# Three of seven replicated tiles of the first chunk made by matmuls with a zero-one matrix instead of transferred

## The reference

```
e = stack([tbl_f[ids[:, f]] for f in range(39)], axis=1)      # 512 x 39 x 16
x0 = xk = e
for W, b in layers:                                            # three layers, 128 wide
    z = relu(einsum('bhd,bkd,hks->bsd', x0, xk, W) + b)
    xk, rest = z[:, :64], z[:, 64:]                            # rest goes to the output
z = sum over d of the rests and of the last z                  # 512 x 256
h = relu([z, dense_ctx] @ W_top1 + b_top1)                     # 512 x 512
y = relu(h @ W_top2 + b_top2) @ W_top3                         # 512 x 1
```

## Time and profile before

| | |
|---|---|
| median of three runs | 650.6 us |
| profiled execution | 650.27 us, span 648.4 us |
| PE busy | 610.6 us (94%), 2008 instructions |
| DVE busy | 562.3 us (87%) |
| POOL busy | 535.9 us (83%) |
| ACT busy | 409.4 us (63%) |
| DMA | 90.30 MB, mean 139 GB/s |

### The profile page before, as it was taken

The page is one execution under the profiler, slowest core; times in us unless marked ns, Lnnn a source line. Parts: engine busy times, 40 slices in busy tenths (PEclk is TensorE's granted clock), DMA queues, the critical chain, the costliest instruction groups (busy, mean ns, idle before and its releaser), DMA issues. The chain is left out here.

```text
span 648.4 us, 6323 instructions
## 1 busy us (share of the span) xinstructions
PE 610.6 (94%) x2008; PEld 377.5 (58%) x2008; DVE 562.3 (87%) x637; ACT 409.4 (63%) x551; POOL 535.9 (83%) x326
## 2 busy tenths in 40 slices
PE   4269899999999999999999999999999999999998
PEld 1126466656666566656656566656666665665554
DVE  1469898998989898998999898998989898988973
ACT  2135758577766758576766758576766758585533
POOL 6778799998989899998989899998989896865550
PEclk9978999999999999999999999999999999999999
DMA  6689554738364655648373546648373545620000
GB/s 228 153 194 272 141 156 100 230 79 247 73 204 107 192 155 132 198 84 247 72 224 83 170 113 131 199 78 252 72 227 90 177 96 140 186 65 1 0 0 2
DMA packets 64044, 90.30 MB, mean 139 GB/s; under 512 B 46624, under 2 KB 49568, under 8 KB 60042
## 3 DMA queue, kind: packets, MB, share of 16 engines
q1 hardware_dynamic: 57506, 88.29, 50.1%
q0 software_dynamic: 5120, 1.29, 2.1%
q10 hardware_dynamic: 1384, 0.32, 0.2%
HBM read 87.31 MB, written 8.95 MB: 148 GB/s over the span
## 5 line engine op out<-in xcount | busy, mean ns | idle before, releaser
L398 POOL TENSOR_TENSOR low<-prod,high 128x1024 fp32r<-128x1024 f32 (+1 forms) x160 | 381.0, 2399 | 54.3 <-ACT high L469 53.0
L643 DVE TENSOR_TENSOR prod<-spread,x 128x1024 f32<-128x1024 f32 x256 | 308.0, 1214 | 32.8 <-ACT x L489 29.1
L759 PE MATMUL z<-prod,w_sb 128*128 128x512 f32 (+2 forms) x608 | 290.8, 599 | 18.6 <-DVE prod L624 14.0
L469 ACT ACTIVATE high<-prod 128x1024 fp32r<-128x1024 f32 (+1 forms) x160 | 168.0, 1058 | 118.1 <-DVE prod L643 100.6
L776 PE MATMUL z<-high,high_w_L 128*128 128x512 f32 (+1 forms) x448 | 203.3, 454 | 5.3 <-ACT high L479 4.3
L791 PE MATMUL z<-low,high_w_L 128*128 128x512 f32 (+1 forms) x448 | 182.8, 489 | 4.3 <-POOL low L398 2.9
L388 POOL DMA_INDIRECT gat<-table_dram,index x160 | 154.0, 962 | 36.5 <-issue 33.9
L776 PE MATMUL z<-high,low_w_L 128*128 128x512 f32 (+1 forms) x448 | 177.9, 397 | 0.0
L759 PEld LDWEIGHTS z<-prod,w_sb 128*128 128x128 f32 (+2 forms) x608 | 115.7, 191 | 105.6 <-issue 85.2
L791 PEld LDWEIGHTS z<-low,high_w_L 128*128 128x128 f32 (+1 forms) x448 | 82.4, 189 | 70.5 <-issue 45.7
L489 ACT ACTIVATE x<-z,bias_sb 64x512 f32<-64x512 f32 (+1 forms) x174 | 112.4, 646 | 13.2 <-PE z L759 6.9
(11 more groups left out here) (48 smaller groups left out, 104.0 us busy)
## 6 DMA issues: line engine op xcount, KB each, us to landing
spread<-x_rows SPq DMA_DIRECT2D x15, 1792.0 KB, 7.2
spread<-x_rows SPq DMA_DIRECT2D x32, 768.0 KB, 12.6
spread<-x_rows SPq DMA_DIRECT2D x16, 1024.0 KB, 7.3
x_rows<-x_rows SPq DMA_DIRECT2D x16, 390.0 KB
x0base<-x_rows SPq DMA_DIRECT2D x47, 78.0 KB
gat<-table_dram,index POOLq DMA_INDIRECT x160, 3.4
x_rows<-gat SPq DMA_DIRECT2D x31, 72.0 KB
wt_sb<-wt_dram SPq DMA_DIRECT2D x2, 512.0 KB, 4.3
```

The costliest lines, as they stand in the source:

```text
L398: pool.tensor_tensor(low[0:rows, h, 0:k, :], prod[0:rows, slot(c, kind, g), 0:k, :], high[0:rows, h, 0:k, :].bitcast(F32), ALU.subtract).t ...
L469: act.activation(high[0:rows, split_slot(c, kind, g), 0:k, :], prod[0:rows, slot(c, kind, g), 0:k, :], ACT.Copy).then_inc(high_ready, 1)
L643: dve.tensor_tensor(prod[0:rows, slot(c, kind, g), :, :], spread[0:rows, c % 2, g, :].unsqueeze(1).to_broadcast([rows, k, N]), x[0:rows, : ...
L759: last = pe.matmul(z[:, :], w[0:rows, at + j, :], prod[0:rows, slot(c, kind, g), j, :], start=g == 0 and j == 0, stop=closes and j == k - 1)
```

## The change

The lot of tiles 0-1 is not transferred, nor is tile 6. `FIRST_CUTS` is now two lots, tiles 2-3 and 4-5. A matrix `select` of zeros and ones (39 rows by three times 117 columns, 54.8 KB) is loaded at the start into a corner of `spread`. After the context matmuls TensorE waits for it, for VectorE to have taken the context sums out of `x1` and `x2`, and for `x0base`, and makes tiles 0, 1 and 6 from the first 39 rows of `x0base` by one matmul each, into `x1` (two halves) and `x2`. VectorE multiplies groups 0 and 3 of the first chunk from there, with `x0base` itself as the other factor in place of its copy `base`.

```diff
-FIRST_CUTS = ((0, 2), (2, 4), (4, T0))
+FIRST_CUTS = ((2, 4), (4, 6))
+SELECTED = (0, 1, 6)
...
+        select_sb = spread[0:F, 1, n1 + n2:G1, :].rearrange("p g n -> p (g n)")[:, 0:len(SELECTED) * R0]
...
+        selected = {t: (x1[0:R0, 0, :], x1[0:R0, 1, :], x2[0:R0, 0, :])[n] for n, t in enumerate(SELECTED)}
...
             def load_base(c, js=range(DPT)):
...
+                    if c == 1:
+                        sp.wait_ge(prod_done, PROD_NUMBER[0, "L0", G0 - 1])
...
             def load_spread(c, p):
...
                 if c == 1 and p == 0:
                     sp.wait_ge(low_w_ready, 3)
+                    sp.wait_ge(select_done, len(SELECTED))
...
             sp.dma_start(bt1_sb[:, :], bt1).then_inc(ctx_in, 16)
+            sp.dma_start(select_sb, select).then_inc(select_in, 16)
             sp.dma_start(w1_part, w1_split).then_inc(w1_in, 16)
...
             def product0(c, g):
-                if g == 0:
+                if g == (1 if c == 0 else 0):
                     dve.wait_ge(base_ready, c + 1)
-                    if c >= 1:
-                        dve.wait_ge(spread0_in, 16 * c)
+                if c >= 1 and g == 0:
+                    dve.wait_ge(spread0_in, 16 * c)
...
+                x0, other = spread0[0:rows, 2 * g:2 * g + k, :], base
+                if c == 0 and 2 * g in SELECTED:
+                    dve.wait_ge(base_in, 16 * DPT)
+                    dve.wait_ge(select_done, 1 + SELECTED.index(2 * g + k - 1))
+                    x0 = x1[0:rows, 0:k, :] if g == 0 else x2[0:rows, 0:k, :]
+                    other = x0base
...
+            pe.wait_ge(select_in, 16)
+            pe.wait_ge(ctx_taken, H1 // P)
+            pe.wait_ge(base_in, 16 * DPT)
+            for n, t in enumerate(SELECTED):
+                pe.matmul(selected[t], select_sb[:, n * R0:(n + 1) * R0], x0base[0:F, :],
+                          start=True, stop=True).then_inc(select_done, 1)
             pe.wait_ge(w1_in, 32)
...
+def selection():
+    out = np.zeros((F, len(SELECTED), R0), np.float32)
+    rows = np.arange(R0)
+    for n, t in enumerate(SELECTED):
+        out[(rows % F + t) % F, n, rows] = 1
+    return out.reshape(F, len(SELECTED) * R0)
```

More of the change, by code:

```diff
@@ L148, in stage_end, with tower_kernel @@
     return max(DONE[c, kind, g] for g in range(G0 if kind == "L0" else G1))
-def tower_kernel(nc, ids, offsets, table, w0a, w0b, w1, w1_split, w2, w2_split, biases, wt1, bt1, wt2, bt2, wt3, ctxT, out):
+def tower_kernel(nc, ids, offsets, table, w0a, w0b, w1, w1_split, w2, w2_split, biases, wt1, bt1, wt2, bt2, wt3, ctxT, select, out):
     with ExitStack() as ctx:
@@ L227, in tower_kernel @@
         ctx_in = sem("ctx_in")
+        ctx_taken = sem("ctx_taken")
+        select_in = sem("select_in")
+        select_done = sem("select_done")
         ctx_done = sem("ctx_done")
@@ L623, in product0 @@
                 rows, k = shape_of("L0", g)
-                dve.tensor_tensor(prod[0:rows, slot(c, "L0", g), 0:k, :], spread0[0:rows, 2 * g:2 * g + k, :],
-                                  base[0:rows, :].unsqueeze(1).to_broadcast([rows, k, N]),
+                x0, other = spread0[0:rows, 2 * g:2 * g + k, :], base
[4 more added lines that the diff above has]
+                    other = x0base
+                dve.tensor_tensor(prod[0:rows, slot(c, "L0", g), 0:k, :], x0,
+                                  other[0:rows, :].unsqueeze(1).to_broadcast([rows, k, N]),
                                   ALU.mult).then_inc(prod_done, 1)
@@ L703, in _ @@
                 dve.wait_ge(ctx_done, m + 1)
-                dve.tensor_scalar(ctx_part[:, m, :], ctx_sum[m], bt1_sb[:, m:m + 1], 0.0, ALU.add, ALU.add)
+                dve.tensor_scalar(ctx_part[:, m, :], ctx_sum[m], bt1_sb[:, m:m + 1], 0.0, ALU.add, ALU.add
+                                  ).then_inc(ctx_taken, 1)
             dve.wait_ge(gathered[0], 16 * GAT)
@@ L913 @@
         "ctxT": a["dense_ctx"].T,
+        "select": selection(),
     }
@@ L921 @@
                                                  "w2_split", "biases",
-                                                 "wt1", "bt1", "wt2", "bt2", "wt3", "ctxT")], out)
+                                                 "wt1", "bt1", "wt2", "bt2", "wt3", "ctxT", "select")], out)
     r = run_bass_kernel_spmd(nc, [arrays], core_ids=[0])
```

## The result

The changed kernel took 648.04 us (median of 7 runs, 646.53 to 649.41), the kernel before 650.51 (7 runs). The ratio is 0.996, with a 95% interval from 0.9949 to 0.9971: faster by 0.4%, 2.5 us, where 3.4 were forecast. The profiled execution took 647.67 us, its span is 645.8 us; PE is busy 614.4 us in it, 3.8 more than before, the three matmuls taking 5.4; the DMA moved 89.64 MB.

The account below looks back on a forecast made before the run. DMA queue, tied with VectorE, bounds the first 60 us. TensorE's 0.2 + 1.77 + 1.5 makes 3.5 us, less 0.1 for uncovered waits: 650.6 - 3.4 = 647.2 us, range 645.9 to 649.3.

Parts of the forecast that it names:

- What bounds it, and the bytes: First 60 us: the DMA queue and, tied with it, VectorE bound; 702 KB fewer ahead save 3.4 to 3.5 us.
- Three matmuls: Before chunk 0's L0: select matmuls start at 23.84, run at the lower clock, first tiles ready at 27.65, TensorE free 28.97.
- TensorE in the stage: Chunk 0's L0: group 0 taken 0.8 us later, yet the stage closes at 36.85 to 37.45; 0.2 us gained.
- Rival D: Chunk 0's L0 stays at the lower clock, closing at 40.1; slower by 1.5 to 2.5 us, 652.6; chance 0.05.
- Chunk 0's L1: VectorE's waits vanish, 3.2 us with chunk 1's; TensorE gains 1.77 idle plus 1.5 clock, 3.5 with L0's 0.2.
- B: Chunk 0's L1: TensorE's clock falls to 0.50 all the same; gain only 2.0 us, 648.6; chance 0.16.
- The 1.5 us for the second fall: Chunk 0's L1: without TensorE's idle gap, the 3 us at half clock from 50 to 53 vanish, saving 1.5 us.
- Rival A: Chunk 0's L0: select matmuls raise the clock, stage closes at 35.5, 1.75 us gained; 646.4; chance 0.15.
- Rival C: Chunk 1: `spread0` still lands at 57.90, so only 0 to 0.8 us of gain is left; 650.2; chance 0.09.

Follow-up runs that it names:

- e1: Changed kernel, but all three lots transferred as before (702 KB more), select matmuls kept; 649.89 us against 649.68 for the kernel before, ratio 1.0001.
- e6: Kernel before the change with twelve unused 128-row matmuls between the context matmuls and L0; 650.16 us against 649.94, ratio 1.0004.
- e3: Changed kernel with the select matrix padded with zeros from 39 to 117 rows; 646.3 us, ratio 0.9938 to the kernel before.
- e7: Changed kernel with select matrix padded to 117 rows and four unused matmuls between chunk 0's L0 and L1; 645.58 us against 649.94, ratio 0.9923.
- e2: Changed kernel with eight unused 128-row matmuls between the context and select matmuls; 646.67 us, ratio 0.9946 to the kernel before.
- e5: Changed kernel without select matrix and matmuls, first chunk's groups 0 and 3 multiplying x0base by itself (values wrong); 647.79 us against 649.94, ratio 0.9959.
- e8: Changed kernel without select matrix and matmuls, groups 0 and 3 multiplying x0base by its PSUM copy (values wrong); 646.49 us against 649.63, ratio 0.9954.

## Why the prediction was right, and where it was not

*What bounds it, and the bytes.* Right. The copy's reader went at 30.07 (30.3 forecast), the second piece at 36.12 (36.1 to 36.8), `spread0` of chunk 1 3.7 us sooner (at most 3.4). e1 puts the bytes back and the gain is gone.

*Three matmuls.* The price by the context matmuls was right: 3.84 us from their start to the first product (3.81), and 5.4 us until TensorE was free (5.1). They started 0.36 later than forecast (24.20), and the third held TensorE until 29.57, which I had at 29.0.

*TensorE in the stage.* This is the term that was mis-sized: I had a close of 36.85 to 37.45 and 0.2 us gained; it was 38.59 in the first trace, 1.34 lost, and 37.38 and 37.67 in the two others, one of them just inside my bounds. I let the clock rise 4.0 us after group 0 or at the same time as before; in the three traces it rose 4.0 to 5.3 us after. Rival D's mechanism, the stage at the lower level nearly throughout, did happen in the first trace, and its point of decision held: the close stayed under 39.6, and e6 shows a close of 40.45 costing next to nothing at the mark, so D's price of 1.5 to 2.5 us was too high. The changed kernel has no such wait left in L1: in its first trace VectorE needs 17.4 us of its own work from the first copy to chunk 1's product, so there a later close costs directly, and even D's 40.1 would have put that product at about 57.6 (an estimate), before the 57.98 of the earlier trace rows.

*Chunk 0's L1.* The waits are right: all three of VectorE's gone, TensorE's gap gone, and TensorE still the last at 60.52 (0.41 us wait). In none of the three traces did the clock fall again in L1, which speaks against B, though the lower level lasted until 46 in the first and until 47 to 48 in the others. The 1.5 us for the second fall is the weak term: it was read off one execution, and e1 has no such fall with the bytes kept. The sum with the stage's true close is -1.34 + 1.77 + 1.5 = 1.9; measured are 2.3 at 60.52. VectorE's rows give it without that term: its first copy is 1.35 later (37.32 to 38.67), waits of 2.34 + 0.27 + 0.40 = 3.01 are gone, its operations overlap so that they take 0.28 less, and its wait for TensorE is 0.36 shorter (0.77 to 0.41). That makes 2.30.

*Rival A.* The select matmuls of 39 rows didn't raise the clock, as the 16-row context in the earlier trace rows had suggested; filled to 117 rows they did (e3, and e7 again), and the time went to 646.3 where A had 646.4. The Trainium skill (TensorE: Matmul & The Clock Gate, Part 1) lets activity release the throttle. The traces agree for matmuls of 117 rows (e3) and 128 rows (e2), and not for 5.4 us of 39 rows or 7.2 us of 16.

*Rival C.* Its mechanism is ruled out: chunk 1's products started at 56.04 without a wait. In the first trace the gain at 60.52 is in the span undiminished. But "from 62.82 on all goes by the engines' own work" left out the clock: in the two other traces of the changed kernel 1.4 us are lost behind the mark. Their gains there, 2.7 and 3.2 us, come nearer to the forecast 3.4 than the medians' 2.5. How the 0.9 us between forecast and measurement divide between the stage's close and this fall is not shown.

## What to carry to other kernels

A transfer avoided early in the queue was worth its bytes to everything behind it here, and more than to its own reader: follow the queue to the next wait. The matmuls that stand in for data movement came when TensorE had idled and was at its lower level, and with few rows they left it there for the work behind them; filling the contraction, with zeros in the weights, cost nothing on TensorE here and brought the upper level. And where a stage's end is covered by a later wait, a loss in it is free until the wait is used up.

## What the runs showed of the hardware

- Six passes of 39 rows (5.44 us) left the next group at the lower level (3.78 us) in four traces; six of 117 rows, of which 78 have zero weights, had it at the upper one (e3: 5.34 and 1.95 us, e7: 4.72 and 1.96).
- The same program's clock rises at different times: 4.0 to 5.3 us after group 0 in three traces of the changed kernel. A fall near 78 us (76 to 86) costs 1.4 us in four of the eleven traces.
- A VectorE product with both operands in SBUF (e5, 23.93 us) lay beside a GpSimd gather of 1.69 us; with one operand in PSUM (e8, 24.41 us) the gather took 0.95. The Trainium skill (SBUF — State Buffer, SBUF: two separate sides) says that VectorE with two SBUF inputs and a GpSimd operation that reads SBUF take one port pair in turns, the one that comes second blocking until the first is done. These two traces agree: the product ended 0.87 us after the gather began, and the gather is 0.74 us longer.
- The tenth gather of chunk 1, issued 0.7 us later in e5, had the stores that wait for it go 4.3 us later. It had come behind the first piece of `spread`; that this is the reason is argued from the order, not tested.
